# Decay differences of a gated delta rule from two half-precision parts instead of full-precision products

## What is computed

```python
beta = sigmoid(xn @ Wb)
g = -exp(A_log) * softplus(xn @ Wa + dt_bias)      # one decay logarithm a token and head
def step(S, xs):                                   # over 1024 tokens or more, per head
    S = S * exp(gt)
    delta = (vt - kt @ S) * bt
    S = S + outer(kt, delta)
    return S, qt @ S
```

## Time and profile before

| | us |
|---|---|
| median of three runs | 866.18 (865.59 to 872.69) |
| the profiled execution | 867.84 |
| its span in the trace | 866.3 |
| mean granted clock of TensorE | 0.956 of full speed |

### The profile page before, as it was taken

How to read it: one execution, slowest core, us unless ns; L and a number is a source line. 1 busy time by engine, 2 the same in 40 slices (tenths; PEclk the granted TensorE clock), 3 DMA queues, 4 the chain that set the end, 5 groups by cost and what they waited for, 6 DMA issues and landing times.

```text
span 866.3 us, 15485 instructions
## 1 busy us (share of the span) xinstructions
PE 775.0 (89%) x5688; PEld 450.5 (52%) x5688; DVE 576.7 (67%) x1400; ACT 470.3 (54%) x1078; POOL 384.7 (44%) x419
## 2 busy tenths in 40 slices
PE   2989378998978999996999997899788999999998
PEld 1455156755537765645775654665233444444443
DVE  4889967768875879795788797567763544444400
ACT  3757736663794764686665487568753333333300
POOL 2376967567694454676464768022441000000000
PEclk9989779998989999899999999999899999999999
DMA  6501020230012023003023001055883422312010
GB/s 202 202 14 38 16 76 33 86 102 7 29 27 93 16 93 98 1 0 120 10 87 88 23 1 34 6 163 121 199 198 103 119 64 73 86 49 73 25 61 36
DMA packets 59937, 62.21 MB, mean 72 GB/s; under 512 B 30392, under 2 KB 45101, under 8 KB 59863
## 3 DMA queue, kind: packets, MB, share of 16 engines
q1 hardware_dynamic: 53526, 44.97, 18.5%
q0 software_dynamic: 4224, 13.11, 4.9%
q10 hardware_dynamic: 2112, 3.15, 1.1%
HBM read 33.69 MB, written 19.73 MB: 62 GB/s over the span
## 4 chain that ended last, share of the span: by engine, by line
PE 58%; DVE 12%; POOL 10%; issue 6%; DMA 5%; SPq 5%; ACT 2%; POOLq 0%; DVEq 0%; ACTq 0%
PE bank L643 14%; PE pd L1980 6%; PE pd L1982 6%; PE pd L1981 6%; SPq L423 5%; DMA dw<-down_rows,member 3%; PE bank L729 2%; DVE cv L1040 2%; PE bank L720 2%; PE bank L803 2%; POOL cv L1627 2%; PE bank L855 2%; POOL rn L1608 1%; PE bank L831 1%; DVE BA L1210 1%
## 5 line engine op out<-in xcount | busy, mean ns | idle before, releaser
L643 PE MATMUL bank<-x_parts,w 128*128 128x512 f16 x576 | 130.0, 384 | 1.5 <-DVE x_parts L997 1.5
L2052 DVE TENSOR_TENSOR hh<-sg,pu 128x512 f32<-128x512 f32 x64 | 43.9, 687 | 95.8 <-ACT sg L2019 90.1
L643 PEld LDWEIGHTS bank<-x_parts,w 128*128 128x128 f16 x576 | 56.2, 99 | 69.3 <-issue 6.4
L1924 POOL DMA_DIRECT2D yr<-y_attn x16 | 8.8, 551 | 185.7 <-DMA out<-yr 185.6
L643 PE MATMUL bank<-w,x_parts 128*128 128x384 f16 x384 | 75.3, 353 | 7.8 <-ACT V L1404 7.6
L2019 ACT ACTIVATE sg<-pg 128x512 f32<-128x512 f32 x64 | 38.0, 594 | 63.2 <-PE pg L1967 63.1
L643 PEld LDWEIGHTS bank<-w,x_parts 128*128 128x128 f16 x384 | 38.6, 105 | 38.1 <-issue 7.9
L1608 POOL TENSOR_TENSOR rn<-t,mhalf 128x6 f32<-128x6 f32 x16 | 22.8, 1422 | 73.1 <-DVE t L1203 73.1
L1040 DVE SCALAR_TENSOR_TENSOR cv<-raw,taps,cv 128x512 f32<-128x512 f32 x72 | 53.5, 809 | 0.0
L1980 PE MATMUL pd<-dw,it 128*128 128x512 f16 x128 | 49.6, 388 | 3.1 <-issue 3.1
L1981 PE MATMUL pd<-dw,it 128*128 128x512 f16 x128 | 49.6, 387 | 0.0
(11 more groups left out here) (310 smaller groups left out, 2054.3 us busy)
## 6 DMA issues: line engine op xcount, KB each, us to landing
xb<-in_x SPq DMA_DIRECT2D x4, 1024.0 KB, 5.7
xr<-in_x SPq DMA_DIRECT2D x16, 256.0 KB, 2.6
y_attn<-xr SPq DMA_DIRECT2D x16, 256.0 KB, 2.2
down_rows<-inv SPq DMA_DIRECT2D x8, 512.0 KB, 5.8
yr<-y_attn POOLq DMA_DIRECT2D x16, 256.0 KB, 2.9
out<-yr SPq DMA_DIRECT2D x16, 256.0 KB, 2.0
xn_hi<-x_parts POOLq DMA_DIRECT2D x4, 512.0 KB
xn_lo<-x_parts POOLq DMA_DIRECT2D x4, 512.0 KB
```

Of the source, the lines that this page charges most:

```text
L643: ins = nc.tensor.matmul(out, a, b, start=first and i == 0, stop=last and i == 2)
L2052: v.tensor_tensor(hh[:, i % 2, :], sg[:, i % 2, :], pu[i % 2][:], ALU.mult).then_inc(h_ready, 1)
```

## The change

The gate values are split into two half-precision parts, once a stage, by a new function `split_g` on POOL (a cast of 24 numbers a token and a subtraction). `masked_g` multiplies both parts with the mask in one instruction of 1536 half-precision elements, into the same bytes as before. `differences` takes four half-precision products of 384 columns where it took two in full precision, with a half-precision copy of the mask `after`. On POOL the masked values of chunk 0 move behind halo 5 and square 3, and the split comes behind square 2.

```diff
+        made(g.tensor_copy(P.after16[:], P.after[:]))
...
+        gm = [t.bitcast(F16).rearrange("p (a h c) -> p a h c", a=2, h=NH) for t in
+              (eg[:, 1].rearrange("p h c -> p (h c)"), X2s[:].rearrange("p a h c -> p (a h c)"))]
+        g_parts = sb("g_parts", [128, 2, NCH, NH], F16)
...
-                    nc.tensor.matmul(ps[:, 0:HALF], P.after[:], gm[c % 2][:, hf:NH:2, :], start=True, stop=True).then_inc(f, 1)
+                    nc.tensor.matmul(ps[:, 0:HALF], P.after16[:], gm[c % 2][:, 0, hf:NH:2, :], start=True, stop=False)
+                    nc.tensor.matmul(ps[:, 0:HALF], P.after16[:], gm[c % 2][:, 1, hf:NH:2, :], start=False, stop=True).then_inc(f, 1)
...
-                g_.tensor_tensor(out=gm[c % 2], in0=P.upto[:].unsqueeze(1).broadcast_to([128, NH, CH]),
-                                 in1=g[:, c, :].unsqueeze(2).broadcast_to([128, NH, CH]), op=ALU.mult).then_inc(gm_ready, 1)
+                g_.tensor_tensor(out=gm[c % 2], in0=P.upto[:].unsqueeze(1).unsqueeze(1).broadcast_to([128, 2, NH, CH]),
+                                 in1=g_parts[:, :, c, :].unsqueeze(3).broadcast_to([128, 2, NH, CH]), op=ALU.mult).then_inc(gm_ready, 1)
+
+            def split_g(s):
+                pool.wait_ge(g_ready, s.val(1, 1))
+                if not s.first():
+                    pool.wait_ge(gm_ready, s.val(NCH, 0))
+                g_.tensor_copy(g_parts[:, 0], g[:]).then_inc(g_split, 1)
+                pool.wait_ge(g_split, s.val(2, 1))
+                g_.tensor_tensor(out=g_parts[:, 1], in0=g[:], in1=g_parts[:, 0], op=ALU.subtract).then_inc(g_split, 1)
+                pool.wait_ge(g_split, s.val(2, 2))
...
                     halo(s, n)
-                    if n == 4:
-                        pool.wait_ge(g_ready, s.val(1, 1))
-                        masked_g(s, 0)
                     if n == 2 and s.idx() == 1:
                         samples.gather(pool, range(12, 13))
                     if n >= 2:
                         square(s, n - 2)
+                    if n == 4:
+                        split_g(s)
+                masked_g(s, 0)
                 masked_g(s, 1)
```

More of the change, by code:

```diff
@@ L565, in attend @@
         E = (eg[:, 0], vT[:, 1:3, :].rearrange("p a c -> p (a c)")[:, 0:NH * CH].rearrange("p (h c) -> p h c", h=NH))
-        gm = (eg[:, 1], X2s[:].rearrange("p a h c -> p (a h c)").rearrange("p (h c) -> p h c", h=NH))
+        gm = [t.bitcast(F16).rearrange("p (a h c) -> p a h c", a=2, h=NH) for t in
+              (eg[:, 1].rearrange("p h c -> p (h c)"), X2s[:].rearrange("p a h c -> p (a h c)"))]
+        g_parts = sb("g_parts", [128, 2, NCH, NH], F16)
         tap_products = (eg[:].rearrange("p a h c -> p (a h c)").rearrange("p (t n) -> p t n", t=TAPS - 1), xb[:, 0:TAPS - 1, :])
@@ L581, in attend @@
         dec_ready, nk_ready, ks_ready = sem("dec_ready"), sem("nk_ready"), sem("ks_ready")
-        gm_ready, a_masked = sem("gm_ready"), sem("a_masked")
+        gm_ready, g_split, a_masked = sem("gm_ready"), sem("g_split"), sem("a_masked")
         taps_ready, tap_step, v_conv = sem("taps_ready"), sem("tap_step"), sem("v_conv")
@@ L1835, in _ @@
             store_y(b, NCH - 1)
-CONSTANTS = 14
+CONSTANTS = 15
 DVE_STEPS = 3 * NQK + 5 + 2
@@ L2447, in __init__ @@
         self.ident, self.ones, self.after, self.upto = (sb(n, [128, 128]) for n in ("ident", "ones", "after", "upto"))
+        self.after16 = sb("after16", [128, 128], F16)
         self.pair = sb("pair", [128, 2])
```

## The result

The changed kernel takes 883.95 us, median of 4 runs (882.68 to 885.05), against 867.95 us (865.59 to 872.69, 4 runs) for the kernel before on the same chip: ratio 1.017, 95% interval 1.013 to 1.021. That is 1.7% slower, 16 us, where the forecast was 0.7% and 5.8 us. The direction was right and the size was not: the time lies outside the range of 862 to 878.

A forecast was written before the change was run, and what follows sets the result against it. TensorE was busiest (89%), but VectorE instructions held beside POOL were taken to decide the convolution stretch. Stages of +0.8, +1.3, +1.4 and +2.4 us made +5.9: 872.0 us, 0.7% slower, range 862 to 878.

The forecast's parts named there:

- Masked product 2.7 us: On POOL: each multiplication of mask and gate values, now 1536 half-precision elements, takes 2.7 us where it took 1.46.
- hold 2.45: On VectorE: an instruction with SBUF inputs stands still 2.45 us beside each new masked product on POOL.
- Multiply-adds near 9.5: On VectorE: the six multiply-adds of each stage's last pair of convolutions take near 9.5 us together.
- First scores 2.7 to 2.9 late: On TensorE: chunk 0's scores come 2.7 to 2.9 us later in the second and third stage.
- Scores of chunks 1 to 3 without gaps in 8.3 us: On VectorE: three chunks' scores and the key tokens run without gaps in 8.3 us, where they took 9.0.
- The split, put at 0.6: On POOL: the two new operations on 24 elements in front of the halo copy take 0.6 us for both.
- Rival 1: POOL's half-precision products do not hold VectorE: -1.6 us a stage for three stages, 861 us, chance 0.15.
- rival 2: POOL's masked product near its lower end, 1.46 us; each stage but the last gains about 0.8: 865 us, chance 0.08.
- rival 3: Masked product of 3.4 us or more, or low clock through chunk 1's scores and chunk 2's differences: 878 us, chance 0.17.
- What is given back: From first scores to inversion: part of the third stage's 2.9 us delay is recovered, scores ending 1.5 us late.
- First stage: +0.8: First stage: scores end 1.3 us late, less 0.5 of cover before a DMA lands and spline work starts: +0.8.
- the clock stays low: On TensorE: low clock through chunk 1's scores and chunk 2's differences costs 1.5 + 0.65 us in three stages, 6.5.

The follow-up runs named there:

- e_short: Changed kernel with POOL's masked product cut to 768 half-precision elements, the high part only: 876.9 us, ratio 1.005 to the kernel before.
- e_ks: Changed kernel with the two small key-factor operations moved from VectorE to POOL, ahead of chunk 2's masked values: 887.1 us, ratio 1.018 to the kernel before.
- a_again: Changed kernel run once more, unaltered, as an anchor: 885.1 us, ratio 1.018 to the kernel before.
- a_sp: Changed kernel with SP's first-stage control-point loads put ahead of the second chunk's down-projection loads: 884.4 us, ratio 1.024 to the kernel before.
- b_pe: Kernel before with only TensorE's differences changed to four half-precision products, POOL's order and 768-element product kept: 871.3 us against 867.1, ratio 1.005.
- a_warm: Changed kernel with extra unread half-precision TensorE products around the first norms, 8 ahead and 4 behind: 887.8 us, ratio 1.025 to the kernel before.
- a_ord: Changed kernel with POOL's old order, split and chunk 0's masked values ahead of the third square: 885.5 us, ratio 1.018 to the kernel before.
- e_long: Kernel before with only POOL's masked product lengthened to 1536 half-precision elements: 880.3 us, ratio 1.012.
- b_order: Kernel before with only POOL's masked values of chunk 0 moved behind its fourth square, in full precision: 873.3 us, ratio 1.007.
- b_warm: Kernel before with two extra unread half-precision TensorE products behind each block's eight norm products, 12 a stage: 872.7 us, ratio 1.004.

## Why the prediction was right and wrong

The mechanism and its price at the place where it was looked for: right. Masked product 2.7 us, measured 2.75 to 3.20; hold 2.45, measured 2.5 (9.04 less the 4.05 of a free pair is 4.99, for two). Multiply-adds near 9.5, measured 9.04. First scores 2.7 to 2.9 late, measured 3.1 to 3.2. Scores of chunks 1 to 3 without gaps in 8.3 us, measured 8.1. The split, put at 0.6, took 0.67. Rival 1 (half precision does not hold VectorE) is refuted by these 9.04 and by e_short's 6.48, rival 2 by 2.75 us, the first half of rival 3 (3.4 us or more) by 3.20 at most. That the product came out at the price taken is in part luck: of 768 elements more each took 1.67 ns, the 1.68 of the step from 256 to 512 elements, and not the 1.5 that was used.

Three steps failed: 5.0, 1.6 and 2.8 us, less 0.5 at the end, make up the 8.9 between forecast (+5.9) and profiled execution (+14.8).

1. "What is given back" was the largest. The prediction had the inversion late by 1.3, 1.4 and 2.4 us, and it came 3.4, 2.8 and 3.9 late, 5.0 more over three stages. Of these, 1.0 lies ahead of the first scores (9.5 us late in the three stages where 8.5 were forecast). The other 4.0 is the return: from the first scores to the inversion 3.4 us less were forecast over the three stages, and it was 0.6 more. It had priced the way from the first scores to the inversion by rows of score instructions alone, which POOL does not hold. Between them stands the small operation on the key factors, in and out in SBUF, 0.17 us before. Its duration is no guide to its risk: what counts is what it waits out, up to the whole of POOL's product. e_ks shows this hold at 2.7, 1.3 and 1.7 us, 5.7 together. The third stage by itself: forecast first scores 350.65, moved by the stage's own delay of 4.84 (g at 336.21 and not 331.37) 355.5, measured 355.81; forecast end of scores 370.7, measured 372.1. 1.4 missing: 0.3 from the first scores, the rest the hold. In the whole time of e_ks this does not show, as its ratio of 1.018 says.

2. "First stage: +0.8" came out as 3.4, less 1.0 in the stretch behind it (layer norm to g): 1.6 too low. a_again has +3.7 and +0.3 there. The cover named there (VectorE ends 0.5 ahead of a DMA) was the wrong one. The path runs from the last value convolution over SP's queue and the spline's inputs to POOL; a_sp moves its start and its end by the same 1.4 to 1.5 us. Asking "who waits for this semaphore" for each queue that it is waited on in, SP's too, would have found it.

3. Nothing was set down for what lies behind the inversion; it cost 2.8 us in the profiled execution (+1.8 and +1.0). This is no fixed term: in a_again, the same kernel, it is 0.1, and the last stretch is 2.0 longer instead. The first two steps are found in both traces (g to inversion +10.1 in each). The inversions have a few lengths, and which comes goes with TensorE's granted clock. From 2 to 6 us behind the start of the inversion it is 0.57 to 0.62 in all ten inversions of 35.1 us or more, 0.67 in the one of 34.5 us, and 1.00 in the other 28 of the thirteen traces. Rival 3 had named "the clock stays low", at the scores. It was low there (2.94 us for those of chunk 0), but in the changed kernel VectorE does not wait for it: its first scores wait for ScalarE (1.89 <-ACT eg), and its later ones follow the held operation without a gap.

TensorE's saving itself is real but was misjudged as a gain: b_pe has it (1.8, 1.6, 0.6) and is still 0.5% slower, at a lower mean clock in its ten executions. What stays open is where the lower clock is paid. Long inversions (35.1 us or more) come in 6 of 9 in b_pe, e_short and e_ks and in 2 of 3 in a_warm, but only in 2 of 12 in the changed kernel, a_again, a_ord and a_sp; with full-precision differences there are none in 15 (the 34.5 of before is the longest). The 2.0 us in a_again's last stretch have no explanation here.

For the parts: POOL's length 1.2% (e_long), TensorE's shorter products 0.5% (b_pe), each within 0.4%. That they add up to the 1.7% is in part chance: the hold of the key factors is not in e_long, and POOL's order reads 0.7% in b_order and nothing within the change (a_ord beside a_again).

## What to carry to other kernels

When an instruction on POOL gets longer, list every VectorE instruction with its operands in SBUF that can fall beside it, the tiniest too, and price each by the length of POOL's instructions beside it and not by its own. Then follow each late semaphore through the queues that wait for it, SP's first. A saving on TensorE counts only to the next place where another engine is the bound, and it can come with a lower granted clock, as in b_pe: compare the mean clock of all executions, not of one trace.

## What the runs showed of the hardware

- A VectorE operation on 24 elements with an SBUF input takes 2.51 us beside a POOL product of 2.75 (0.17 otherwise), 1.21 beside one of 1.47 (e_short), and 3.38 over a gather issued by POOL and the product of 2.76 behind it.
- The scores, whose first operand is in PSUM, take 2.43 to 2.44 us for six beside POOL's products of 2.75 as without them.
- POOL's product takes 1.47 us for 768 and 2.75 for 1536 half-precision elements undisturbed, which is 1.67 ns for each of the 768 more. Half-precision output brings nothing.
- Half-precision in place of full-precision differences lowered the mean granted clock of a whole execution from 0.956 to 0.945 (b_pe, ten executions).
- Extra wide products between narrow ones did not raise the clock at the scores behind them (b_warm: 2.94 us in every stage, although TensorE does not wait there in the third).
- TensorE's granted clock over a stretch may go from 0.86 to 0.91 and leave its length the same to 0.01 us.
